# A graph transformer block: the last stage's three norms in one chain over five parts of two tiles

## What is computed

```python
h = xn
for l in range(2):
    h_new = gatv2_layer(h, ...)              # elu(sum of alpha * source rows), 8 heads
    h = layer_norm(h_new + h, ln_w[l], ln_b[l])
x = x + layer_norm(h, on_w, on_b) + mix(xn)
x = x + gelu(_layernorm(x) @ in_weight.T + in_bias) @ out_weight
```

## Time and profile before

| what | before |
|---|---|
| median of 3 runs (lowest, highest) | 2679.82 us (2678.9, 2687.27) |
| profiled execution: its own time, its span | 2676.28 us, 2674.6 us |
| the last stage in it | 2485 to 2674.6, 189.6 us |
| TensorE, VectorE, ScalarE busy in the stage | 119.6, 106.1, 83.2 us |
| first normalized tile starts (ScalarE) | 2527.36 |
| loads of ScalarE's function tables in the stage | 7 (4 before a Gelu, 3 before an exponential) |
| small steps on VectorE in the stage | 12 chains of 12 steps, 4 shifts |
| all transfers, 2505 to 2510, 2510 to 2515 | 111 GB/s, 0 |

### The profile page before, as it was taken

One profiled execution on the slowest core, in us unless ns is written; L12 is line 12 of the kernel. 1 busy time (PEld: TensorE's weight loads), 2 busy tenths in 40 slices (PEclk: granted clock), 3 DMA queues, 4 the chain that ended last, 5 costly groups with the idle time before them and its releaser, 6 DMA issues. The chain is left out here.

```text
span 2674.6 us, 91791 instructions
## 1 busy us (share of the span) xinstructions
PE 2300.7 (86%) x32401; PEld 1764.1 (66%) x32402; DVE 1732.8 (65%) x4402; ACT 1135.1 (42%) x2703; POOL 837.8 (31%) x749
## 2 busy tenths in 40 slices
PE   6998887994999999999996797699999999999376
PEld 4664454653777777787774464587777777877365
DVE  4227873334777777777776633577777777777664
ACT  2000010032555555565554213355555555555453
POOL 0000010002555555555550000455555555543000
PEclk9999988997999999999998999899999999999698
DMA  4001033125777777677672112677777777765200
GB/s 162 0 1 63 9 99 137 50 66 159 214 211 208 211 213 213 202 213 213 201 209 77 67 47 71 196 216 215 207 213 211 208 208 212 212 202 157 113 30 29
DMA packets 141991, 397.65 MB, mean 149 GB/s; under 512 B 24584, under 2 KB 79147, under 8 KB 141619
## 3 DMA queue, kind: packets, MB, share of 16 engines
q0 software_dynamic: 58432, 298.63, 38.4%
q1 hardware_dynamic: 81709, 93.29, 11.0%
q10 hardware_dynamic: 1764, 4.60, 0.5%
HBM read 368.18 MB, written 16.78 MB: 144 GB/s over the span
## 5 line engine op out<-in xcount | busy, mean ns | idle before, releaser
L465 POOL DMA_INDIRECT at_rows<-table,at_index x728 | 829.0, 1139 | 1233.4 <-DVE at_index L671 856.3
L484 ACT ACTIVATE at_relu<-at_turned,at_attn_size 128x512 f32<-128x512 f32 x1092 | 731.2, 691 | 695.8 <-PE at_turned L544 627.2
L544 PE MATMUL at_turned<-ident,at_rows 128*128 128x128 f32 x4368 | 828.0, 280 | 0.0
L542 PE MATMUL at_turned<-at_place,dst_rows 96*128 96x128 bf16 x4368 | 796.9, 223 | 25.5 <-ACT at_relu L484 13.5
L544 PEld LDWEIGHTS at_turned<-ident,at_rows 128*128 128x128 f32 x4368 | 629.4, 144 | 47.6
L542 PEld LDWEIGHTS at_turned<-at_place,dst_rows 96*128 x4368 | 455.9, 106 | 71.1 <-issue 66.1
L667 DVE SCALAR_TENSOR_TENSOR sums<-sums,at_factor,at_total 128x97 f32 x1456 | 352.7, 311 | 218.8 <-PE at_total L578 111.6
L578 PE MATMUL at_total<-at_rows,at_spread 128*32 128x100 f32 x11648 | 336.5, 253 | 51.4 <-issue 43.6
L578 PEld LDWEIGHTS at_total<-at_rows,at_spread 128*32 128x32 f32 x11648 | 270.1, 110 | 102.7 <-issue 78.7
L657 DVE TENSOR_TENSOR at_spread<-at_lined,at_weight 128x1024 f32<-128x1024 f32 x182 | 223.4, 1227 | 114.5 <-ACT at_weight L494 99.1
L634 DVE SCALAR_TENSOR_TENSOR at_relu<-at_relu,at_pair_sign 128x512 f32<-128x512 f32 x364 | 256.6, 746 | 18.1 <-ACT at_relu L484 18.1
(11 more groups left out here) (288 smaller groups left out, 2711.7 us busy)
## 6 DMA issues: line engine op xcount, KB each, us to landing
at_place<-local_rows SPq DMA_DIRECT2D x182, 96.0 KB
at_rows<-table,at_index POOLq DMA_INDIRECT x728
at_flags<-run_flags SPq DMA_DIRECT2D x182, 64.0 KB
dst_rows<-pr_parts SPq DMA_DIRECT2D x240, 48.0 KB, 1.9
table<-pr_src_row SPq DMA_DIRECT2D x20, 400.0 KB, 2.3
mx_w<-in_L_mix_W_qkv SPq DMA_DIRECT2D x2, 2304.0 KB, 19.0
pr_w_src<-in_L_gnn_Wsrc SPq DMA_DIRECT2D x2, 2304.0 KB, 9.9
x_mix<-mx_nodes_t ACTq DMA_DIRECT2D x10, 384.0 KB, 2.3
```

What stands on the lines that cost most here:

```text
L465: pool.indirect_dma_start(rows[b][:, j, :], None, table, bass.IndirectOffsetOnAxis(index[b][:, j:j + 1], 0)).then_inc(gathered[b], 16)
L484: act.activation(relu[c][:], turned[chunk(b, c)][:], ACT.Relu, scale=attn_size[:, c:c + 1]).then_inc(bent, 1)
L542: pe.matmul(into, dst_rows[:, bass.ds(at[j], 1), c * P:(c + 1) * P].rearrange("p o d -> p (o d)"), place[b][:, j * P:(j + 1) * P], start=T ...
L544: last = pe.matmul(into, rows[b][:, j, c * P:(c + 1) * P], ident[:], is_transpose=True, start=False, stop=True)
```

## The change

`RowNorms` replaces `RowNorm`: one set of tiles holds the columns of several norms, and `scales(step, turn)` runs one chain over all that are due. The sums of squares of part g of norm number `kind` are kept in row g + kind, so that a turn's chain takes the settled norm of part `turn`, the summed norm of part `turn - 1` and the scaled norm of part `turn - 2`, at most six columns at once. The last stage has five parts of two tiles and nine turns, -2 to 6. In a turn VectorE closes a part, sums up the one before, adds the tiles of the next and takes those of the one after, and ends with the chain for the turn to come. TensorE moves the quarters of a part two turns ahead of its closing. The outputs of a part are computed from turn g + 2, where the even tile's output is computed, and in the turn after it the odd tile's; their adds stand in turn g + 3. The number of passes over whole tiles stays the same. In SyncE's queue the two loads for `Settle` now stand ahead of the input weights, and `y` is loaded in five pieces, not four; the weight transposes stand later. `turnover` uses the same class with one norm, in its old order.

```diff
-    def scales(self, step):
-        dve = step.engine
-        step(dve.tensor_scalar(self.var[:], self.spread[:], 1.0 / D, LN_EPS, ALU.mult, ALU.add))
...
+    def place(self, ap, t, kind):
+        for g, (first, n) in enumerate(self.parts):
+            if first <= t < first + n:
+                at = kind * self.width + t - first
+                return ap[:, g + kind, at:at + 1]
...
+    def scales(self, step, turn):
+
+        dve, here = step.engine, [kind for kind in range(self.kinds) if 0 <= turn - kind < len(self.parts)]
+        low, high = here[0] * self.width, here[-1] * self.width + self.parts[turn - here[-1]][1]
+        var, work, spread, rstd = self.var[:, low:high], self.work[:, low:high], self.spread[:, turn, low:high], self.rstd[:, turn, low:high]
+        step(dve.tensor_scalar(var, spread, 1.0 / D, LN_EPS, ALU.mult, ALU.add))
...
-LAST_PARTS = ((0, 3), (3, 3), (6, 2), (8, 2))
+LAST_PARTS = tuple((t, 2) for t in range(0, NT, 2))
...
+                settle.load(sp)
                 sp.dma_start(w_in_rows[:], in_weight.rearrange("(c p) n -> p c n", p=P)).then_inc(w_in_loaded, 16)
...
+                for turn in range(-2, TURNS):
+                    if turn == 1:
+                        turn_weights()
+                    if turn == 2:
+                        act.wait_ge(w_out_loaded, 32)
+                    out_of, close_of = tiles(turn - SCALED), tiles(turn)
+                    for t in out_of:
+                        normalize(t)
+                    for i in range(2):
+                        for t in out_of[i:i + 1]:
+                            copy_turned(t)
+                        for t in close_of[i:i + 1]:
+                            square_h(t)
+                    for t in out_of[0:1]:
+                        gelu(t)
+                    for t in tiles(turn - SUMMED):
                         square_y(t)
...
+                    for t in tiles(turn + 1):
+                        settle.square(act, t)
+                    for t in tiles(turn + 2):
+                        settle.bend(act, t)
+                    for t in out_of[1:2]:
+                        gelu(t)
...
+                for turn in range(-2, TURNS):
+                    moving = tiles(turn + 2)
+                    if turn < SCALED:
+                        for t in moving:
+                            settle.move(pe, t)
+                        if turn == 0:
+                            turn_weights()
+                    else:
+                        one, two = tiles(turn - SCALED)
+                        turn_node(one)
+                        turn_node(two)
+                        hide(one)
+                        for t in moving[0:1]:
+                            settle.move(pe, t)
+                        if turn == SCALED:
+                            pe.wait_ge(w_out_loaded, 32)
+                        hide(two)
+                        if one:
+                            put_out(one - 1)
+                        for t in moving[1:2]:
+                            settle.move(pe, t)
+                        put_out(one)
+                put_out(NT - 1)
...
+                def scale(turn):
+                    for t in tiles(turn)[1:2]:
+                        dve.wait_ge(settle.squared, t + 1)
+                    for t in tiles(turn - SUMMED)[1:2]:
+                        dve.wait_ge(h_squared, t + 1)
+                    for t in tiles(turn - SCALED)[1:2]:
+                        dve.wait_ge(y_squared, t + 1)
+                    norms.scales(step, turn)
+                    for t in tiles(turn - SCALED)[0:1]:
+                        step(dve.tensor_tensor(shift[:, t:t + 2], norms.centre[:, SCALED * NT + t:SCALED * NT + t + 2],
+                                               norms.rstd[:, turn, 2 * SCALED:2 * SCALED + 2], ALU.mult))
+                        dve.sem_inc(scaled, 1)
+
+                for turn in range(-2, TURNS):
+                    closing, summing, done = tiles(turn), tiles(turn - SUMMED), tiles(turn - SCALED - 1)
+                    if turn == 0:
+                        dve.wait_ge(settle.loaded, 32)
+                    for t in closing[0:1]:
+                        settle.shrink(dve, t)
+                        settle.shrink(dve, t + 1)
+                        settle.close(dve, t, norms.total_of(t, SUMMED))
+                        settle.close(dve, t + 1, norms.total_of(t + 1, SUMMED))
+                        centre_h(t)
+                        centre_h(t + 1)
+                    for t in done[0:1]:
+                        add(t)
+                    if turn == SUMMED:
                         dve.wait_ge(gain_loaded, 16)
...
+                    for t in summing[0:1]:
+                        dve.wait_ge(y_loaded[t // 2], 16)
+                        shrink_h(t)
+                        shrink_h(t + 1)
                         sum_up(t)
...
+                        sum_up(t + 1)
+                        centre_y(t)
+                        centre_y(t + 1)
+                    for t in tiles(turn + 1):
+                        settle.add(dve, t)
+                    for t in tiles(turn + 2):
+                        settle.take(settling, t)
+                        settle.lift(dve, t)
+                    for t in done[1:2]:
                         add(t)
...
+                    if 0 <= turn + 1 < TURNS:
+                        scale(turn + 1)
+                for t in tiles(len(LAST_PARTS) - 1):
```

More of the change, by code:

```diff
@@ L1407, with __init__ @@
 class Settle:
[L1410 to L1411 removed]
+    def __init__(self, nc, sb, psum, name, layer, sums, nodes, ident, ln_w, ln_b, norms):
+        self.norms, self.parts = norms, norms.parts
         self.layer, self.sums, self.nodes, self.ident, self.ln_w, self.ln_b = layer, sums, nodes, ident, ln_w, ln_b
@@ L1417, in __init__ @@
         self.inverse = sb(name + "_inverse", [P, H])
-        self.norms = [RowNorm(sb, f"{name}_norm{g}", n) for g, (_, n) in enumerate(parts)]
         self.moved_ps = psum
@@ L1466, in lift @@
         dve.scalar_tensor_tensor(self.nodes[:, t, :], self.mean[t % 2][:], 0.0, self.nodes[:, t, :], ALU.max, ALU.add).then_inc(self.lifted, 1)
-    def norm_of(self, t):
-        for g, (first, n) in enumerate(self.parts):
-            if first <= t < first + n:
-                return self.norms[g], t - first
     def add(self, dve, t):
-        norm, i = self.norm_of(t)
         dve.wait_ge(self.exp_done, t + 1)
@@ L1511, in part @@
                 behind[t]()
-        self.normalize(step, g, closed, totals)
-    def normalize(self, step, g, closed=None, totals=None):
-        dve = step.engine
-        first, n = self.parts[g]
         if g == 0:
@@ L1519, in normalize @@
         dve.wait_ge(self.squared, first + n)
-        self.norms[g].scales(step)
+        self.norms.scales(step, g)
         self.shrink(dve, first)
@@ L1768, in finish, with tiles @@
         y_loaded = ctx.enter_context(signals(nc, [f"fi_y_loaded{g}" for g in range(len(LAST_PARTS))]))
-        norm_h, norm_y = ([RowNorm(sb, f"fi_{name}{g}", n) for g, (_, n) in enumerate(LAST_PARTS)] for name in "hy")
-        settle = Settle(nc, sb, moved_ps, "se", LAYERS - 1, sums, nodes, ident, ln_w, ln_b, LAST_PARTS)
-        def part_of(t):
-            for g, (first, n) in enumerate(LAST_PARTS):
-                if first <= t < first + n:
-                    return g, t - first
-        def column(ap, t):
-            i = part_of(t)[1]
-            return ap[:, i:i + 1]
+        norms = RowNorms(sb, "fi_norms", LAST_PARTS, 3)
+        settle = Settle(nc, sb, moved_ps, "se", LAYERS - 1, sums, nodes, ident, ln_w, ln_b, norms)
+        SETTLED, SUMMED, SCALED = range(3)
+        TURNS = len(LAST_PARTS) + SCALED
+        def tiles(part):
+            return range(2 * part, 2 * part + 2) if 0 <= part < len(LAST_PARTS) else ()
         with nc.Block() as block:
@@ L1902, in put_out @@
                     for half in range(2):
+                        if half and moving is not None:
+                            settle.move(pe, moving)
                         for c in range(HC):
@@ L1919, in _, with turn_weights @@
[L1919 to L1940 removed]
+                def turn_weights():
+                    pe.wait_ge(w_in_loaded, 16)
+                    for c in range(HC):
+                        if c:
+                            pe.wait_ge(w_ready, c)
+                        for n in range(KC):
+                            last = pe.transpose(turned[:, n * P:(n + 1) * P], w_in_rows[:, c, n * P:(n + 1) * P], ident[:])
+                        last.then_inc(w_turned, 1)
+                    pe.wait_ge(w_ready, HC)
@@ L1997, in _ @@
-                for t in range(LAST_PARTS[-1][0], NT):
+                def scale(turn):
[10 more added lines that the diff above has]
+                        dve.sem_inc(scaled, 1)
```

191 lines of the change are left out of this document (48 added, 143 removed).

## The result

The changed kernel takes 2660.73 us in the median of four runs (2659.36 to 2663.52), against 2679.53 for the kernel before, measured with it (four runs, 2678.9 to 2687.27). The ratio is 0.9925, interval 0.9905 to 0.9944: faster, by 18.8 us. The forecast was 2657. The profiled execution took 2659.36 us with a span of 2657.7; before, 2676.28 and 2674.6.

What follows compares the result with a forecast made beforehand. Waits for the norms' serial path, not a full engine, were taken to bound the last stage. Losing 10.8 us in filling and winning 33.4 behind it gave 22.6 us less, 2657.2 on the median's scale, range 2651 to 2667.

Steps and rivals of the forecast that it cites:

- a filling that ends after 2541: Sign that the prediction is wrong: first normalized tile later than 2541 us on the profiled clock, against about 2538 forecast.
- none of the four table loads that go was on the path: ScalarE's function-table loads, last stage: seven fall to three, 1.28 us each, and the four dropped delayed nothing.
- Unit costs: VectorE's pieces of work, last stage: take a tile 2.4 us, add 1.06, chain 2.4 at any width, closing 4.0.
- Phase 1: Filling, turns -2 to 1: VectorE sets the pace, first normalized tile at 2538.2, costing 10.8 us once.
- Phase 2: Turn 2, the dear one: TensorE starts slowly at 2539.3, tile 2 is normalized at 2560.8, TensorE resumes at 2561.9.
- I count no loss of clock here: End of turn 2: TensorE's 2.5 us of idleness since output 0 was taken not to lower its clock.
- rival 1: End of turn 2 slips 2 to 3 us, idleness passes 3.88, lower clock costs 5.5; gain 17, 2662.7; chance 0.12.
- rival 4: Higher clock for more of turn 2 and fast moves in turns 0 and 1; gain 26 to 28, about 2653; chance 0.09.
- Phase 3: Turns 3 to 6: TensorE sets the pace at full clock, 19.7 us a turn, 78.8 for four.
- 0.4 us to spare: Turns 3 to 6: TensorE's wait and output, 5.0 us, cover the 4.6 from odd tile's add to transposes.
- Rival 3: Turns 3 to 6: 4.6 us gaps stay and each drops the clock, 7.3 a turn; 6.6 slower, 2686.4; chance 0.03.
- Rival 2: Turns 3 to 6: gaps of 4.6 us stay, turns 24.3 each; gain 4.2, 2675.6, no measurable change; chance 0.08.

Runs made afterwards that it cites:

- e5_old_order_five: Kernel before in its old order, with five parts of two tiles instead of four parts, without the pipeline; 2716.49 us, ratio 1.0035 to before.
- e3_two_buffers: Changed kernel with quarters going alternately to two PSUM tiles, all moved before the first transposes; 2651.86 us, ratio 0.9903 to before.
- e4_keep_clock: Changed kernel, with TensorE moving tile 9's quarters a second time, unread, in its idle time before turn 3; 2660.6 us, ratio 0.9931 to before.
- e2_three_chains: Changed kernel with a separate two-column chain for each norm at the same places, 15 chains instead of 7; 2683.89 us, ratio 1.0014 to before.
- e7_add_same_turn: Changed kernel with each output added in the turn that makes it, ahead of the next chain; 2713.33 us, ratio 1.0028 to before.
- e1_after: The changed kernel run again, unchanged; 2661.31 us, ratio 0.9934 to before.
- e6_chain_first: Changed kernel with the chain written ahead of the odd tile's add, not behind it; 2684.77 us, ratio 0.9917 to before.
- e8_three_buffers: e3_two_buffers plus outputs and odd transposes using the second PSUM tile, chain before odd add, tile 1's Gelu after normalizing tiles 2 and 3; 2667.76 us, ratio 0.9854.

## Why the prediction was right, and the step that failed

**Direction and size.** The changed kernel was forecast at 2657, faster by 22.6 us, and measured at 2660.73, faster by 18.8. On the profiled execution the forecast was 2653.7 and the time 2659.36, 5.7 us more: 3.4 for the stage's later start, 2.1 for the stage (160.9 instead of 2647.0 - 2488.2 = 158.8), 0.2 for the tail. The 2.1 are 0.9 in turn 2 and 1.4 in turn 3, and little elsewhere. The sign "a filling that ends after 2541" was met to the letter (2541.44) and the last add came at 2651.53, not near 2647; counted from the start of the stage the filling ended as worked out.

**What bounds the kernel before.** Waits for the norms' serial path: right. e5_old_order_five, which keeps that order, has 5.64 and 4.61 us of idleness before its last two parts, the two lengths of the earlier trace rows. One reading was wrong: that none of the four table loads that go was on the path. In the trace of before VectorE waits for a pass of ScalarE that stood behind such a load (2541.60 to 2542.89), and its next chain stands behind that:

```profile
2543.77 0.96 DVE L1477 SCALAR_TENSOR_TENSOR nodes<-se_bent,nodes 128x768 f32<-128x768 f32 x1 [1.14 <-ACT se_bent L1462]
```

No run shows what this 1.1 us was worth in the end, and the sum did not use it.

**Unit costs.** Right. The chain of six columns runs from 2538.71 to the shift at 2541.13, 2.42 us against 2.4.

**Phase 1.** Right to 0.15 us: from the first quarter to the first normalized tile 49.82 measured, 49.97 worked out. The transposes follow 1.08 after it, out of idleness. e3_two_buffers shows that the waits for quarters belong to this path. The agreement is closer than the term deserves, since other executions scatter by up to 2.5 us here with the level of the clock (e4_keep_clock): that the first execution hit it to 0.15 is luck.

**Phase 2.** 22.6 worked out, 23.47 measured. From the first transposes to the first output it was 16.2 and is 17.01; behind it, to the normalizing of tile 2, it was 5.3 and is 5.37. So the slow start lasted longer than in the earlier trace rows: the two tiles' hidden products took 6.08 and 4.29 us, 10.37 together against the 9.38 of the working. ScalarE was last by 0.2 us, as walked: it normalizes at 2564.90, and VectorE's shift (2564.39, and 0.31 for the hand-over as at 2541.13) would have let it do so at 2564.70. It went from load to pass without a gap:

```profile
2558.19 1.28 ACT L1487 ACT_TABLE_LOAD   x1
2559.49 0.84 ACT L1487 ACTIVATE se_bent<-se_bent 128x768 f32<-128x768 f32 x1
...
2562.84 1.28 ACT L1835 ACT_TABLE_LOAD   x1
2564.14 0.89 ACT L1835 ACTIVATE fi_hidden<-fi_hidden_ps,fi_bias 128x128 f32<-128x128 f32 x3
2564.90 1.95 ACT L1822 ACTIVATE nodes<-fi_y,fi_shift,fi_norms_rstd 128x768 f32<-128x768 f32 x2
...
2624.87 1.95 ACT L1822 ACTIVATE nodes<-fi_y,fi_shift,fi_norms_rstd 128x768 f32<-128x768 f32 x2 [2.54 <-DVEq L1969]
```

The page of the Trainium skill (ScalarE: Activation LUTs, section on what ACT_TABLE_LOAD costs), which adds a drain of some 1.38 us, does not hold in these rows either: the next pass starts 0.02 us after the load.

**The step that failed** is the sentence "I count no loss of clock here" about the 2.5 us of idleness ahead of turn 3. The idleness was well sized (2.32), its consequence was not. The precedent it leaned on was one wait of 3.42 that left output matmuls at full speed. Here, six transposes and the 0.99 for the copy after a wait of 2.32, the clock was down: 1.51 and 9.00 instead of 0.84 and 8.20. The turn so took 21.13 us instead of the 19.7 worked out. e4_keep_clock took 1.5 us of the idleness away and the 1.4 us with it. This is the clock's part of rival 1 at half its price (1.4 of 2.7), in a wait that its bound of 3.88 had excluded. The other term that was too small is turn 2's, by the 0.9 us above. What rival 4 hoped for did not come: turn 2 had less of the higher level than walked, and the moves of turns 0 and 1 took 2.81 us.

**Phase 3.** 19.7 a turn worked out, 19.65 and 19.66 measured. The 0.4 us to spare were right: ahead of turn 6 the normalizing starts at 2624.87, so the transposes could follow 1.1 us later, at 2626.0; TensorE comes from its second output at 2626.43, without a wait. e2_three_chains and e7_add_same_turn show from both sides how narrow that is: 4.8 us more of VectorE before the normalizing, or an add with no work of TensorE's own behind it, and the gaps are back.

**The rivals.** Rival 3's mechanism is real and its price of 7.3 us a turn was right: the turns of e7_add_same_turn are 6.8, 7.2 and 7.4 above 19.65 in turns 3 to 5. That it ends 7.0 us behind before, where rival 3 had 6.6, is in part luck: its stage is only 4.3 us longer than that of before (185.63 against 181.36). Rival 2, the gaps without the clock, is in none of these traces: after every gap of 4.6 ahead of a part, TensorE's next work ran slow. Its chance should have gone to rival 3.

**The later start.** That the stage began 3.4 us later was in no term. Up to there the kernels differ in `turnover` alone, by the class of its norms, and perhaps in where tiles lie in memory. In the first set the changed order and its variants begin at 2491.6, 2490.6, 2489.8, 2489.8 and 2491.1, the one execution of before at 2488.2. In the second the old order (e5_old_order_five) begins at 2522.6, the three variants of the new one at 2521.4, 2516.3 and 2520.4, that is, not later. The traces say where the time arose: VectorE's first step on `at_sign_mask` (line 709) of the second layer, at the start of the edges' work, stands at 1684.07 before, 1684.92 after, and 1683.80 and 1683.68 in e1_after and e3_two_buffers. From there to the last stage it is 804.2 us before, 806.7 after, and 806.8, 803.8, 806.2 and 805.2 in the other four of that set. So at least 2.5 of the 3.4 us lie in the edges' stage, whose instructions are the same, and one kernel with the new class is faster there than before. I take it for chance; that is argued from these ten starts and not shown.

## What to carry to other kernels

When norms or other chains of small steps sit between matmuls, pack the chains of several stages of a pipeline into one, since a step's cost hardly depends on its width (0.16 to 0.17 us on 2 to 8 columns here), and let TensorE have at least as much to do behind the last input of the chain as the way through the chain takes; here 4.6 us from add to transposes against 5.0, a wait of 1.1 and an output of 3.9. Then price each idle stretch with the clock that it takes along (4.6 us of waiting cost 7.2). Filling a short one with matmuls nobody reads gave 1.4 us back in the trace; in the time of the whole kernel it could not be seen. When the waits are gone, look at the PSUM tiles: letting idle ones double as second buffers was worth almost as much again as the whole change, 17 us on the way from e6_chain_first to e8_three_buffers, though the one change of order on ScalarE in e8_three_buffers was not measured apart.

## What the runs showed of the hardware that I had not expected

Which waits take the clock along. These are the idle stretches ahead of a part's first transposes in turns of the new order from the third on, and what followed; behind the first transposes stands the 0.99 for the copy in every row but that of e8_three_buffers. Six transposes take 0.82 to 0.88 at the higher level and 1.51 to 1.54 at the lower.

| kernel | idle, us | first transposes | second | hidden products |
|---|---|---|---|---|
| e4_keep_clock | 0.84 | 0.88 | 0.85 | 8.20 |
| e2_three_chains | 1.73 | 0.88 | 0.85 | 8.20 |
| after (e1_after, e6_chain_first) | 2.32 | 0.88 | 1.51 | 9.00 (8.94, 9.05) |
| e8_three_buffers | 2.57 | 1.40 | 1.49 | 8.89 |
| e2_three_chains | 4.10 | 1.01 | 1.51 | 10.18 |
| e7_add_same_turn, turn 3 | 4.66 | 1.54 | 1.51 | 8.86 |
| e7_add_same_turn, turns 4 to 6 | 4.66, 4.62, 4.61 | 1.54 | 1.51 | 9.26, 9.47, 9.60 |
| e3_two_buffers | 4.76 | 1.54 | 1.51 | 8.91 |
| e2_three_chains | 6.76 | 1.54 | 1.51 | 9.64 |

The wait of 1.73 took nothing; that of 2.32 did, in all three executions that have it, and the fall comes in the work behind the wait. Neither where it falls nor how long it lasts follows the length: the first transposes took 1.40 after 2.57, with no second wait behind, but 1.01 after 4.10; that wait has the dearest hidden products of all, and four waits of nearly the same 4.6 us have products from 8.86 to 9.60. A wait of 3.42 ahead of an output even took nothing. So the cost cannot be read off one wait alone, as the prediction did; what decides it exactly stays open.
